# Moving low parts, a diagonal and a bias lookup between engines in the first mixture of a four-layer block

## What is computed

```
x = x + tanh(g_xattn[0]) * mlstm(layernorm(x), ctx, ctx, ...)
x = x + tanh(g_ffn[0])   * ffn0(layernorm(x), Wr, br, W1, b1, W2, b2)

def ffn0(x, Wr, br, W1, b1, W2, b2):      # 8 experts, hidden width 512
    logits = x @ Wr.T + br
    e = argmax(logits)                    # one expert for each token
    h = relu(x @ W1[e].T + b1[e])
    return h @ W2[e].T + b2[e]
```

## Time and profile before

| what | value |
|---|---|
| median of 3 runs | 650.97 us (648.37 to 651.58) |
| the profiled execution's own time | 647.32 us |
| its span, first to last instruction | 645.5 us |
| PE, DVE, ACT, POOL busy | 565.9, 520.5, 338.9, 251.1 us |
| mean granted clock of PE | 0.958 |

### The profile page before, as it was taken

The page is one execution under the profiler, slowest core; times in us unless marked ns, Lnnn a source line. Parts: engine busy times, 40 slices in busy tenths (PEclk is TensorE's granted clock), DMA queues, the critical chain, the costliest instruction groups (busy, mean ns, idle before and its releaser), DMA issues.

```text
span 645.5 us, 16288 instructions
## 1 busy us (share of the span) xinstructions
PE 565.9 (88%) x5385; PEld 289.1 (45%) x5385; DVE 520.5 (81%) x1135; ACT 338.9 (52%) x667; POOL 251.1 (39%) x464
## 2 busy tenths in 40 slices
PE   4996899996986889985999999999999779996997
PEld 2442368743663335542344433434434324553443
DVE  6795976686898968866799999999999796776886
ACT  4775367664563523443455555555555554333654
POOL 3377010110485048875234344443434200225462
PEclk9997899997998889997999999999999999997999
DMA  8204010041000000000566666656566100001110
GB/s 309 83 2 131 0 69 3 2 118 35 3 4 1 0 4 2 2 2 13 142 170 174 165 179 179 173 166 181 168 164 169 61 2 2 2 2 31 33 52 34
DMA packets 34752, 48.89 MB, mean 76 GB/s; under 512 B 6860, under 2 KB 26904, under 8 KB 34056
## 3 DMA queue, kind: packets, MB, share of 16 engines
q1 hardware_dynamic: 34264, 47.40, 26.1%
q10 hardware_dynamic: 432, 0.73, 0.3%
HBM read 47.29 MB, written 0.82 MB: 75 GB/s over the span
## 4 chain that ended last, share of the span: by engine, by line
PE 44%; DVE 38%; ACT 7%; POOL 4%; issue 4%; DMA 1%; DVEq 0%; ACTq 0%; SPq 0%; POOLq 0%
PE PS L226 28%; DVE PS L1056 9%; DVE SHARED L1205 5%; DVE SHARED L1699 3%; DVE PS L1069 3%; ACT SHARED L1034 2%; PE PS L1342 2%; PE PS L1931 2%; DVE MB L1825 2%; ACT SHARED L1005 2%; PE PS L1937 2%; PE PS L1803 2%; PE PS L737 2%; DVE REC L1945 1%; DVE PS L1825 1%
## 5 line engine op out<-in xcount | busy, mean ns | idle before, releaser
L226 PE MATMUL PS<-XH,UH 128*128 128x512 f16 x232 | 89.8, 387 | 6.7 <-DVE PS L1056 3.3
L1034 ACT ACTIVATE SHARED<-PS 128x512 f16<-128x512 f32 x96 | 57.1, 597 | 71.5 <-DVE PS L1069 67.8
L226 PE MATMUL PS<-XL,UH 128*128 128x512 f16 x232 | 89.2, 385 | 0.0
L226 PE MATMUL PS<-XH,UL 128*128 128x512 f16 x232 | 89.2, 384 | 0.0
L1912 ACT ACTIVATE SHARED<-PS 128x512 f32<-128x512 f32 x96 | 52.1, 594 | 63.6 <-PE PS L226 48.8
L226 PE MATMUL PS<-SHARED,DNH 128*128 128x512 f16 x232 | 69.0, 379 | 4.6 <-DVE SHARED L1205 4.6
L1205 DVE TENSOR_TENSOR SHARED<-PS,SHARED 128x512 f16<-128x512 f32 x96 | 62.1, 687 | 6.8 <-ACT SHARED L1034 3.4
L1005 ACT ACTIVATE SHARED<-PS 128x512 f32<-128x512 f32 x96 | 57.2, 597 | 17.7 <-PE PS L226 15.4
L963 POOL CAST DNH<-DF 128x128 f16<-128x128 f32 x58 | 19.6, 337 | 116.9 <-DMA DF<-in_down 101.3
L1069 DVE TENSOR_TENSOR PS<-PS,SHARED 128x512 f32<-128x512 f32 x92 | 59.7, 694 | 3.7
L1056 DVE TENSOR_TENSOR PS<-SHARED,PS 128x1024 f32<-128x1024 f32 x46 | 56.5, 1229 | 6.7 <-PE PS L226 0.7
(11 more groups left out here) (334 smaller groups left out, 1281.4 us busy)
## 6 DMA issues: line engine op xcount, KB each, us to landing
SHARED<-w_rows_dram SPq DMA_DIRECT2D x31, 384.0 KB, 3.6
SHARED<-w_rows_dram SPq DMA_DIRECT2D x30, 256.0 KB, 3.8
UF<-in_up SPq DMA_DIRECT2D x58, 128.0 KB, 3.4
SHARED<-w_rows_dram SPq DMA_DIRECT2D x31, 128.0 KB, 2.7
DF<-in_down SPq DMA_DIRECT2D x58, 64.0 KB, 2.9
V<-in_up SPq DMA_DIRECT2D x2, 1024.0 KB, 9.8
V<-in_down SPq DMA_DIRECT2D x2, 1024.0 KB, 5.1
SHARED<-t_values_dram SPq DMA_DIRECT2D x2, 1024.0 KB, 10.4
```

The costliest lines, as they stand in the source:

```text
L226: last = pe.matmul(dst, l, r, start=start and i == 0, stop=stop and i == len(pairs) - 1)
L1034: act.activation(HHI[:, u, hf, :], bank(4 + hf) if m == 1 else HF[:, hf, :], ACT.Copy).then_inc(sem("e_high"), 1)
```

## The change

- Low parts of W1: DVE makes none of them in the recurrence any longer. POOL makes quarters 0, 1 and 2 once `next_pool` of the last block is through (semaphore `s_w_pool`); DVE makes quarter 3 in the mixture, behind `pick_dve(1)` (semaphore `s_w`).
- SP's load of W2's first half waits for POOL's quarters 0 and 1, its load of the second half for POOL's quarter 2 and DVE's quarter 3.
- Low parts of W2: all four by DVE, behind `pick_dve(2)`.
- `DIAG`: eight ACT instructions (eye times a scale taken from `R_POS`) in place of one DVE instruction. They stand in ACT's program behind `weights_act(1, q)` and `route_turn_act`, ahead of `gather_act(0)`.
- The biases `B1S`: b1 is loaded as [8, 512]; DVE makes a one-hot [8, 16] in one instruction ahead of `pick_dve(0)`, PE multiplies (four products of 16 columns), ACT copies out 64 columns.
- POOL's zeroing of MB, WRH and WRL moves from the start of the mixture to the start of the recurrence, beside that of CW.
- The first run of fills in the mixture has 10 products, not 12.
- The semaphore `v_in` is merged into `n_exp`.

```
-        def weights_dve(dve, n, q):
-            dve.wait_ge(sem("s_w_high"), 4 * n + q + 1)
+        def weights_low(eng, n, q):
+            eng.wait_ge(sem("s_w_high"), 4 * n + q + 1)
             hi, lo = (w[:, quarter(q), :].rearrange("p e n -> p (e n)") for w in ((W1H, W1L), (W2H, W2L))[n])
-            dve.tensor_tensor(lo, WSTAGE[:, 1024 * q:1024 * q + 1024], hi, ALU.subtract).then_inc(sem("s_w"), 1)
+            signal = "s_w_pool" if n == 0 and q < 3 else "s_w"
+            eng.tensor_tensor(lo, WSTAGE[:, 1024 * q:1024 * q + 1024], hi, ALU.subtract).then_inc(sem(signal), 1)
...
             next_dve(dve, NB - 2)
-            weights_dve(dve, 0, 0)
-            weights_dve(dve, 0, 1)
             next_dve(dve, NB - 1)
-            weights_dve(dve, 0, 2)
-            weights_dve(dve, 0, 3)

         def mlstm_pool(pool):
-            pool.wait_ge(sem("n_exp"), 1)
+            pool.wait_ge(sem("n_exp"), 2)
             pool.tensor_scalar(ENT, ENT, 1e-6, None, ALU.add).then_inc(sem("n_eps"), 1)
-            pool_zeros(pool, 5)
+            for b in range(4, 8):
+                pool_zeros(pool, b)
...
         def moe0_sp(sp):
             for q in range(2):
-                sp.wait_ge(sem("s_w"), 2 * q + 2)
+                sp.wait_ge(sem("s_w_pool"), 2 + q)
+                if q == 1:
+                    sp.wait_ge(sem("s_w"), 1)
                 sp.dma_start(WSTAGE[:, 2048 * q:2048 * q + 2048], t["down0"][:, 2048 * q:2048 * q + 2048])\
                     .then_inc(sem(f"ld_w{q}"), 16)
...
         def bias_dve(dve):
+            dve.tensor_scalar(R_OH, R_EX[0:E0], 1 / 128, SLOT[0:E0, 0:1], ALU.mult, ALU.is_equal).then_inc(sem("r0_step"), 1)
+
+        def bias_pe(pe):
+            pe.wait_ge(sem("r0_step"), EXPERTS + 1)
+            for c in range(4):
+                last = pe.matmul(bank(1)[:, 16 * c:16 * c + 16], B1[:, 128 * c:128 * c + 128], R_OH, start=True, stop=True)
+            last.then_inc(sem("s_ranks"), 1)
+
+        def bias_act(act):
+            act.wait_ge(sem("s_ranks"), 2)
+            act.activation(B1S, bank(1)[:, 0:64], ACT.Copy).then_inc(sem("s_copied"), 1)
...
-        def diag_dve(dve):
-            dve.tensor_tensor(DIAG, over(EYEH[:], NB), along(R_POS, 128), ALU.mult).then_inc(sem("r0_step"), 1)
+        def diag_act(act):
+            act.wait_ge(sem("r0_step"), POSITIONS)
+            for b in range(NB):
+                act.activation(DIAG[:, b, :], EYEH[:], ACT.Copy, scale=R_POS[:, b:b + 1]).then_inc(sem("s_copied"), 1)

         def place_pe(pe):
-            pe.wait_ge(sem("r0_step"), DIAGONAL)
+            pe.wait_ge(sem("s_copied"), 2 + NB)
...
         def moe0_pe(pe):
-            fill_pe(pe, 4, 12)
+            fill_pe(pe, 4, 10)
             ranks_pe(pe)
             route_turn_pe(pe, 0)
             fill_pe(pe, 4, 12)
+            bias_pe(pe)
             pe.wait_ge(sem("r0_step"), EXPERTS)
...
             act.wait_ge(sem("ld_late"), 16 * len(LATE))
             route_turn_act(act, 0)
+            diag_act(act)
+            bias_act(act)
             gather_act(act, 0)
...
         def moe0_dve(dve):
             rows_dve(dve)
             places_dve(dve)
+            bias_dve(dve)
             pick_dve(dve, 0)
-            diag_dve(dve)
             pick_dve(dve, 1)
-            weights_dve(dve, 1, 0)
-            bias_dve(dve)
+            weights_low(dve, 0, 3)
             pick_dve(dve, 2)
-            for q in (1, 2, 3):
-                weights_dve(dve, 1, q)
+            for q in range(4):
+                weights_low(dve, 1, q)
...
             if m == 0:
-                for b in (4, 6, 7):
-                    pool_zeros(pool, b)
+                for q in range(3):
+                    weights_low(pool, 0, q)
                 for b in range(4):
-                    pool.wait_ge(sem("s_w"), 5 + b)
+                    pool.wait_ge(sem("s_w"), 2 + b)
                     pool_zeros(pool, b)
```

More of the change, by code:

```diff
@@ L91, in gated_mix_program @@
         VE, RSTD = sb("VE", [128, NB]), sb("RSTD", [128, NB])
-        B1 = sb("B1", [128, CH0])
+        B1 = sb("B1", [E0, F0])
         B2F, B2H, B2L = sb("B2F", [E0, D]), sb("B2H", [E0, D], fp16), sb("B2L", [E0, D], fp16)
@@ L196, in gated_mix_program @@
         TRI, STEP, SLOT = XQT[:, 0:2, :], QX[:, 0].rearrange("p j s -> p (j s)"), REC[:, 0:32]
-        B1S = REC[:, 32:32 + 4 * TILES]
+        B1S = REC[:, 32:96]
         YH, YL = ATH, ATL
@@ L207, in gated_mix_program @@
         R_SUM8, R_EXI = piece(7680 + 504, 2), piece(7680 + 506, 2, i32)
-        R_OH = piece(7168, TILES * E0).rearrange("p (t e) -> p t e", e=E0)
-        R_B1 = piece(6656, 4 * TILES * E0).rearrange("p (t c e) -> p t c e", c=4, e=E0)
+        R_OH = piece(7168, 16, parts=E0)
         WB = [piece(at, 1024) for at in (8192, 9216)]
@@ L301, in values_act @@
             act.activation(VP.rearrange("p b h d -> p (b h) d")[:, :, 0:DH0],
-                           CTOK.rearrange("p (n d) -> p n d", d=DH0), ACT.Copy).then_inc(sem("v_in"), 1)
+                           CTOK.rearrange("p (n d) -> p n d", d=DH0), ACT.Copy).then_inc(sem("n_exp"), 1)
         def gate_weights_dve(dve):
@@ L641, in values_pe @@
             if n == 0:
-                pe.wait_ge(sem("v_in"), 1)
+                pe.wait_ge(sem("n_exp"), 1)
                 pe.wait_ge(sem("g_in"), 2)
@@ L662, in out_pe @@
             if b == 0:
-                pe.wait_ge(sem("n_exp"), 1)
+                pe.wait_ge(sem("n_exp"), 2)
             if b >= 1:
@@ L1217, in gated_mix_program @@
         ROUTED = 2 * NB + 2
-        EXPERTS, DIAGONAL = ROUTED + 13, ROUTED + 14
+        POSITIONS, EXPERTS = ROUTED + 8, ROUTED + 13
         GATHER = ((2, 3), (4, 5), (6, 7), (6, 7))
@@ L1316, in place_act @@
         def place_act(act):
-            act.wait_ge(sem("s_ranks"), 2)
+            act.wait_ge(sem("s_ranks"), 3)
             for i in range(2):
@@ L1326, in put_dve @@
             else:
-                dve.wait_ge(sem("s_copied"), 4)
+                dve.wait_ge(sem("s_copied"), 5 + NB)
             dve.tensor_scalar(PUT[:, i % 2, :], PLACE, SLOT[:, i:i + 1], None, ALU.is_equal).then_inc(sem("s_put"), 1)
@@ L1336, in gather_pe @@
             if c == 2:
-                pe.wait_ge(sem("s_copied"), 4)
+                pe.wait_ge(sem("s_copied"), 5 + NB)
             if c == 3:
@@ L1358, in tile_up_pe @@
             if i == 0:
-                pe.wait_ge(sem("s_w"), 4)
+                pe.wait_ge(sem("s_w_pool"), 3)
+                pe.wait_ge(sem("s_w"), 1)
             if i >= 2:
@@ L1371, in tile_relu_act @@
             if i == 0:
-                act.wait_ge(sem("r0_step"), DIAGONAL + 6)
+                act.wait_ge(sem("s_copied"), 3 + NB)
             if i >= 2:
@@ L1376, in tile_relu_act @@
                 act.activation(RH[i % 2][:, 128 * c:128 * c + 128], bank(2 + i % 2)[:, 128 * c:128 * c + 128], ACT.Relu,
-                               bias=B1S[:, 4 * i + c:4 * i + c + 1]).then_inc(sem("s_relu"), 1)
+                               bias=B1S[:, 16 * c + i:16 * c + i + 1]).then_inc(sem("s_relu"), 1)
             act.wait_ge(sem("s_relu"), 4 * i + 4)
@@ L1390, in tile_down_pe @@
             if i == 0:
-                pe.wait_ge(sem("s_w"), 8)
+                pe.wait_ge(sem("s_w"), 5)
                 pe.wait_ge(sem("s_rows"), 4)
@@ L2426, in _layout @@
     r["gb"] = np.stack([np.tile(a[f"L0_xattn_{g}gate_b"], 16) for g in "if"], axis=1)
-    r["b1"] = a["L0_ffn_b1"].reshape(CH0, 128).T
+    r["b1"] = a["L0_ffn_b1"]
     r["b2"] = a["L0_ffn_b2"]
```

## The result

The changed kernel takes 657.47 us (median of 4 runs, 656.04 to 659.16), the kernel before in the same session 649.67 (4 runs, 647.80 to 651.58). The ratio is 1.013, 95% interval 1.0094 to 1.0166: slower by 8 us. The profiled execution took 659.16 us with a span of 656.3.

A forecast was written before the change was run, and what follows sets the result against it. Bound: POOL's `NMR` held by DVE's low parts, then DVE's picks, then PE alone. Terms: -3.5 up to gather 0, +8.4 wait, +2.65 clock, sum +7.6 on median 650.97, stated as 658.5 us; range 653.0 to 662.0.

The forecast's parts named there:

- The recurrence: Before the mixture: both long `NMR` drop to 0.27 us, -3.75; PE's last turn at full clock starts sooner, -0.4.
- POOL's low parts: Behind the recurrence: three parts at 2.28 us, 6.8 in all; DVE's cast or one-hot choice waits for the third, +1.2.
- Ranks and fills, zeroings: Ahead of gather 0: two fills less remove DVE's wait for ranks, -0.7; zeroings moved to the start cost nothing.
- The new wait: Between gather 0 and place: PE waits for ACT's diagonals, queued behind the second load of down weights, +8.4 us.
- the first paragraph: Reading of today's bounds: ACT ends its four W2 high parts at 66.7, then waits 7.32 us for gather 0.
- The clock: In gather 1: PE's clock is low after the wait, so it takes 6.1 us, not 3.45: +2.65.
- Behind gather 1 the order is the old one: From gather 1 to the kernel's end: nothing is tied to a fixed time, so the shift stays.
- rival 3: At place: ACT's wait never reaches PE, diagonals done by 75.2; the gain of 3.5 us stays, 647.5; chance 0.06.
- Rival 4: In the mixture's tiles: 7 us are taken back, no change, 651; chance 0.08 together with the mildest ends of 1.
- 1: Same wait, milder: DVE unhindered by POOL, diagonals 0.26 us, gather 1 at full clock; +3.45, 654.4; within the wait's 0.86.
- 2: Same wait, heavier: POOL 2.5 us each, diagonals 0.40, place and gather at half clock; +10.45, 661.4; within the wait's 0.86.

The follow-up runs named there:

- the first experiment: The changed kernel with ACT's high parts of W2's quarters 2 and 3 moved behind the place copies: 648.6 us, ratio 0.9998 to the kernel before.

## Why the prediction was right, step by step

**Forecast and result.** 658.5 was forecast, with 653.0 to 662.0 for the range; it is 657.47. The mechanism is the one that was named, and the first experiment shows it by removal. That the total agrees is in part luck: the mixture alone was forecast 1.5 us too slow (7.6 against 6.1), and 1.9 us came from a place at which nothing was expected. The base was off as well, by 1.3 us: 650.97 was the median of three runs, and the kernel before takes 649.67 beside the changed one. As a difference, 7.6 was forecast and 7.8 measured.

**The recurrence (-3.75, -0.4).** Right. The last `NMR` ends at 56.74 against 59.75; with the 0.74 of the first load that is 3.75. The last turn starts at 57.32 against 60.73, 4.15 with the 0.74, and the four fills ahead of the turns took 1.03 us, as at full clock.

**POOL's low parts (6.8 us, +1.2).** They took 2.1 us each, 6.29 in all, below my lower estimate of 2.28. So DVE's cast waited 0.6 us and not 1.2. That the running POOL operation holds it is shown by a third part less (0.17), by a fourth more (2.09 on the next operation), and by the cast's end, which follows the third part's in every kernel. The rule that the prediction cites from the Trainium skill (SBUF — State Buffer, section "SBUF: two separate sides") agrees with these for the one-hot choice. The cast has one input; the page has such an operation in the lock only in a two-port mode, and no run here shows in which mode it ran.

**Ranks and fills, zeroings (-0.7, 0).** The ranks end before DVE asks, as forecast. POOL waits 0.92 us for DVE behind the four zeroings, so they delay nothing. Gather 0 starts at 69.94, 69.2 without the 0.74; I had 69.9. The cast's shorter wait is the difference. That gather 0 then took the 5.31 us of the forecast is luck, since other profiles have it at 3.63 to 6.58.

**The new wait (+8.4).** Each member of the chain came within 0.3 us: the load 5.33 (5.1 forecast), two high parts 2.00 (1.95), CT 1.00 (1.02), diagonals 2.43 (2.4), PE idle 8.60 (8.4). The moments agree too, load from 73.20 (73.1), diagonals done at 83.8 (83.6), but with help: the 0.74 of the first load and the cast's 0.6 cancel. One reading of the first paragraph is wrong, without effect on the sum: ACT does not wait 7.32 us right behind its high parts; the earlier trace rows has 2.02 us, then CT, then the 7.32.

**The clock (+2.65).** The step was mis-sized in its parts. Gather 1 took 4.98 and not 6.1, as the clock came back at 88, when PE had done place and about half of gather 1's products. Place took 1.03 and not 0.45, since it was the first to meet the low clock. Together 6.01 against 6.55, which had place at full clock. The experiment with fills gives 2.0 as the clock's worth.

**"Behind gather 1 the order is the old one, ... so the shift stays to the end".** This step failed. Gather 1 ends 7.25 us later (89.87 against 82.62), 6.5 without the 0.74, and the mixture 6.1: 0.4 is given back in the tiles. Then the loop of the second mixture adds 1.9, although no instruction of it had changed, and what goes with it is that ACT's program ahead of it was 9 instructions longer. I had no row for that, and looked for none.

**The rivals.** The other side (rival 3) was right in its condition: the diagonals must be done when gather 0 ends. ACT's new order makes that so, and the mixture then ends 3.6 us sooner than before, near the rival's 3.5, but by other parts: gather 0 starts 4.9 us sooner (68.54 against 73.41) and took 1.7 us less, by its clock, and some is lost again to ACT's later stand. Against the second profile of the kernel before (131.08, gather 0 at 3.63 too) it is 2.6 us. The loop takes 1.9 of that back, and the median is that of before. With all four low parts on POOL the load itself lands as early as the rival asks (69.68, it asks for 69.8), and PE does not wait. Rival 4 fell, as only 0.4 us was taken back. Each term of 1 and 2 came out between its bounds: DVE's wait for POOL 0.6 us (0 to 1.9), the eight diagonals 2.43 us in all (2.4 was forecast), the low clock 2.1 us by the two groups of products (0 to 3.9).

## What to carry to other kernels

When work is moved to another engine to free a wait, follow the buffer that it releases: here the load of the next weights hung on the last low part, and that part had gone behind 4.2 us of picks. In an engine's program nothing that is needed soon may stand behind an instruction that waits for a far transfer; of two repairs, moving the waiting instructions gave 8.9 us; making their data come sooner gave 3.1 us where it brought the load one pick forward, and 9.8 us where it took DVE out of the load's way. So bring the data forward by enough, or move what waits; both together were best (-12.7, with the diagonal on DVE). After any change in an early stage, compare the period of the long loops behind it, for a loop of 23 passes took back 1.9 us here though its own instructions were the same.

## What was not expected of the hardware

- **A loop's period goes with the number of instructions that ACT has ahead of it.** Every second chunk takes 4.23 us with 365 and 366 activations and 4.31 with 374, and eight empty instructions switch it (with a small tile more, which moved others by 32 bytes). One more on DVE does not. Why it is so was not tested, nor any other count.
- **Full and half clock in the same stretch of the same program.** Gather 0 took 5.31 us in the profile of after and 3.63 in the kernel with the low part sooner, though PE had the same program up to there and 1.03 us of idle time before it in both. With 1.03 or 1.04 us of idle time other profiles had 5.05, 5.17, 6.53 and 6.58. In the first three chunks of the second mixture it was 15.54 and 18.88 for the unchanged kernel. A difference of 1.7 or 3.3 us between two single profiles at such a place says nothing of a change.
- **POOL on a wide tile** is faster than its smaller shapes suggest: 2.1 us for 128x1024, from float32 to float16, where two sizes below it pointed to 2.28.
